# Two graph and mixture-of-experts layers: where the second choices are sent, and how the experts' tiles are cut

## The reference, cut to what matters

```
x = x + gnn0(layernorm(x), adj)     # in the eigenbasis of the adjacency's Laplacian
x = x + ffn0(layernorm(x))          # 8 experts, silu(x w1) * (x w3), then w2; top 2 by softmax
x = x + gnn1(layernorm(x), adj)     # graph convolution, two batch norms
x = x + ffn1(layernorm(x))          # a shared expert, and 8 experts with gelu and biases; top 2
```

## Time and profile before

| | |
|---|---|
| median of 3 runs | 1472.82 us (1469.61 to 1474.72) |
| the profiled execution | 1468.22 us, its span 1466.4 us |
| busy: PE, DVE, POOL, ACT | 77%, 62%, 45%, 38% of the span |
| chain of what ended last | PE 48%, issue 32%, another core or an unknown queue 7%, DVE 6% |
| costliest groups | write-backs L1462 (284 instructions, 300.9 us), sends L1016 (256, 257.7 us) |
| mean granted clock of PE | 0.922 |

### The profile page before, as it was taken

The page is one execution under the profiler, slowest core; times in us unless marked ns, Lnnn a source line. Parts: engine busy times, 40 slices in busy tenths (PEclk is TensorE's granted clock), DMA queues, the critical chain, the costliest instruction groups (busy, mean ns, idle before and its releaser), DMA issues.

```text
span 1466.4 us, 24078 instructions
## 1 busy us (share of the span) xinstructions
PE 1125.4 (77%) x6500; PEld 934.2 (64%) x6500; DVE 902.9 (62%) x3796; ACT 550.2 (38%) x1613; POOL 653.2 (45%) x675
## 2 busy tenths in 40 slices
PE   4555686388727978899999677999878877799990
PEld 3555575266615856688888443776657766699990
DVE  5776789767763544456676778887614433355673
ACT  3556567045511211122222365554323322244440
POOL 3000000054566666665444840044546666656664
PEclk9999999999958998899999798899989988899995
DMA  9993000001112222222242600011112222222436
GB/s 230 428 427 146 1 1 1 0 1 34 37 48 70 72 63 62 64 65 60 84 119 70 229 18 15 5 34 33 39 45 66 68 62 64 62 68 70 131 104 229
DMA packets 59270, 125.58 MB, mean 86 GB/s; under 512 B 13132, under 2 KB 39637, under 8 KB 57600
## 3 DMA queue, kind: packets, MB, share of 16 engines
q0 software_dynamic: 20000, 73.21, 13.2%
q1 hardware_dynamic: 39136, 50.84, 12.9%
HBM read 50.83 MB, written 74.99 MB: 86 GB/s over the span
## 4 chain that ended last, share of the span: by engine, by line
PE 48%; issue 32%; another core or an unknown queue 7%; DVE 6%; ACT 2%; DMA 2%; SPq 2%; POOL 1%; DVEq 0%; POOLq 0%; ACTq 0%
PE bank L1619 15%; PE bank L1610 9%; PE bank L1608 6%; PE bank L1607 6%; PE bank L1828 3%; PE bank L1836 3%; PE bank L1787 2%; PE bank L1595 2%; DMA u<-planes 1%; DVE bnh L1684 1%; PE bank L861 1%; SPq L2148 1%; DVE bn L1123 1%; ACT pay L1903 1%
## 5 line engine op out<-in xcount | busy, mean ns | idle before, releaser
L1462 POOL DMA_INDIRECT planes<-work,goal x284 | 300.9, 1059 | 211.0 <-DVE work L1531 124.2
L1016 POOL DMA_INDIRECT rows<-pay,slot x256 | 257.7, 1007 | 245.4 <-issue 78.3
L1619 PE MATMUL bank<-pay 128*128 128x128 f32 (+1 forms) x1988 | 297.7, 290 | 66.1 <-issue 34.0
L1619 PEld LDWEIGHTS bank<-pay 128*128 128x128 f32 (+1 forms) x1988 | 272.4, 199 | 95.3 <-issue 44.4
L1579 ACT ACTIVATE pay<-bank,pay 128x256 f32<-128x256 f32 x284 | 127.1, 475 | 211.3 <-PE bank L1610 123.9
L1575 ACT ACTIVATE pay<-bank 128x256 f32<-128x256 f32 (+1 forms) x213 | 81.1, 383 | 301.7 <-PE bank L1608 224.1
L1610 PE MATMUL bank<-pay 128*128 128x256 f32 x568 | 145.5, 402 | 3.0 <-issue 1.6
L1552 DVE TENSOR_TENSOR pay<-pay,bank 128x256 f32<-128x256 f32 (+1 forms) x213 | 88.6, 418 | 86.6 <-ACT pay L1575 44.5
L1607 PE MATMUL bank<-pay 128*128 128x256 f32 (+1 forms) x426 | 134.2, 398 | 7.6 <-issue 7.0
L1608 PE MATMUL bank<-pay 128*128 128x256 f32 (+1 forms) x426 | 131.7, 392 | 0.0
L195 PE MATMUL bank<-u 63*64 63x2 f32 (+61 forms) x496 | 73.7, 255 | 67.2 <-DVE u L180 66.1
(11 more groups left out here) (416 smaller groups left out, 2013.2 us busy)
## 6 DMA issues: line engine op xcount, KB each, us to landing
rows<-pay POOLq DMA_DIRECT2D x10, 3432.0 KB, 56.3
pay<-rows SPq DMA_DIRECT2D x142, 130.0 KB
u<-planes SPq DMA_DIRECT2D x64, 256.0 KB, 5.0
planes<-work,goal POOLq DMA_INDIRECT x284
wreg<-in_w SPq DMA_DIRECT2D x1, 4264.0 KB, 24.4
wreg<-in_w SPq DMA_DIRECT2D x1, 4112.0 KB, 13.3
X<-in_x SPq DMA_DIRECT2D x2, 2048.0 KB, 20.0
rows<-pay,slot POOLq DMA_INDIRECT x256
```

Source lines behind the costliest of these rows:

```text
L1016: return self.nc.gpsimd.indirect_dma_start(out=xs, out_offset=bass.IndirectOffsetOnAxis(ap=self.t["slot"][:, k, q:q + 1], axis=0), in_=sel ...
L1462: nc.gpsimd.indirect_dma_start(out=planes, out_offset=bass.IndirectOffsetOnAxis(ap=t["goal"][:, j * 2 + h:j * 2 + h + 1], axis=0), in_=t[" ...
L1619: ins = T.matmul(ps[4 + j % 2][:, h * P:(h + 1) * P], t["hh"][c][0:n, h * P:(h + 1) * P], t["wst"][j % 2][0:n, at + c * P:at + (c + 1) * P ...
```

## The change

- **The table's layout.** Each expert now owns `CAP` = 16640 rows. First choices go upwards from its middle (`CAP * e + 8192`), second ones downwards below it (their slots are counted negative and turned round in `place`). So second slots are final at once, `second_slots` is gone, and `clear_rows` has 20 blocks for 10.
- **The second sends.** They no longer belong to `experts_pool`. The new `send_seconds` marks a group (iota, copy, wait) and sends its 8 x 128 rows. In layer 1 two of them are sent behind each group of firsts from the second on (`BESIDE`); all that remain, 64 in layer 0 and 50 in layer 1, follow the last group at once. `experts_pool` then only writes back, one tile after another as they are ready, with `LANES` = 8 semaphores for 3 and `RING` = 16 for 18.
- **The tiles.** 57 tiles have 256 rows of one expert, 11 are split: two halves of 128 rows, of two experts. That is `NT` = 68 tiles and `NS` = 79 weight sets, for which `wst` has 4 buffers (`WAYS`). The order is 25 tiles of first choices, the 11 split ones, the other 32. A split tile has two row loads, two weight copies, twice the up products on half the columns, and in layer 1 two gelus and two bias additions for one. `table` is rewritten for the new list, with rounding by a large number in place of the 768-wide comparison.
- **The early plane** is fetched from tile `EARLY` = 62 on, with 8 semaphores for 4; what doesn't fit into the loop is fetched and added behind it.

```diff
-NT = (2 * TOKENS + E8 * (TS - 1)) // TS
-CAP = TOKENS + TS
+WHOLE = -(-(2 * TOKENS - E8 * (TS - 1)) // TS)
+MIXED = (2 * TOKENS + E8 * (P - 1)) // P - 2 * WHOLE
+MIXED += MIXED % 2
+NT = WHOLE + MIXED // 2
+NS = WHOLE + MIXED
+FIRSTS = (TOKENS + E8 * (TS - 1)) // TS + 1 + MIXED // 2
+CAP = 2 * TOKENS + TS
...
-BLOCKS = 10
-EARLY = 54
-RING = 18
-FREE = 8
-SENDS = 3
-BEHIND = 14
+BLOCKS = 20
+EARLY = 62
+RING = 16
+LANES = 8
+WAYS = 4
+BESIDE = (0, 2)
...
+    def send_seconds(self, pool, count, xs):
+        for q in range(self.seconds, min(N, self.seconds + count)):
+            g, first = divmod(q, GQ)
+            if first == 0:
+                pool.wait_ge(self.s(f"sent{g}"), 16 * GQ * (self.layer + 1))
+                qs = slice(q, q + GQ)
+                self.nc.gpsimd.iota(self.t["payi"][:, qs, P], ...).then_inc(self.s("marked"), 1)
+                self.nc.gpsimd.tensor_copy(self.t["pay"][:, qs, P + 1], self.t["gate2"][:, qs]).then_inc(...)
+                pool.wait_ge(self.s("marked"), self.past("marked", 2 * (g + 1)))
+            self.send(q, 1, xs).then_inc(self.s("sent_second"), 16)
+            self.seconds = q + 1
...
     for g in range(GROUPS):
         route.scatter(pool, g, xs, ready, rest)
+        if g:
+            route.send_seconds(pool, BESIDE[0], xs)     # BESIDE[1] in gnn1_pool
+    route.send_seconds(pool, N, xs)
...
+def split(j):
+    return PURE <= j < PURE + MIXED // 2
...
-    j = 0
-    if route.split:
-        pool.wait_ge(S("route_second"), sum(SPLIT[:layer + 1]))
-        route.mark_second(pool)
-        for q in range(FREE):
-            route.send(q, 1, xs).then_inc(S("route_sent_second"), 16)
-        for k in range(-(-(N - FREE) // SENDS)):
-            pool.wait_ge(s("xt"), past("xt", k + 1))
-            for q in range(FREE + k * SENDS, min(N, FREE + (k + 1) * SENDS)):
-                route.send(q, 1, xs).then_inc(S("route_sent_second"), 16)
-            if k >= BEHIND:
-                give_back(j)
-                j += 1
-        while j < k:
-            k += 1
-            pool.wait_ge(s("xt"), past("xt", k + 1))
-            give_back(j)
-            give_back(j + 1)
-            j += 2
-    for j in range(j, NT):
+    for j in range(NT):
         give_back(j)
...
     def weights(j):
-        expert = dve.value_load(t["expert"][j:j + 1, 0:1], min_val=0, max_val=E8 - 1)
-        if j >= 2:
-            dve.wait_ge(s("down"), past("down", j - 1))
+        for n in sets_of(j):
+            expert = dve.value_load(t["expert"][n:n + 1, 0:1], min_val=0, max_val=E8 - 1)
+            if n >= WAYS:
+                dve.wait_ge(s("down"), past("down", tile_of(n - WAYS) + 1))
...
+        for k, set_no in enumerate(sets_of(j)):
+            w = t["wst"][set_no % WAYS]
+            to = slice(k * P, (k + 1) * P) if split(j) else slice(0, TS)
+            ins = T.matmul(ps[c][0:n, to], w[:, a:a + n], x[:, to], start=True, stop=True)
...
     finish(NT - 1)
+    for T in range(NT - EARLY - 1, TILES):
+        add_plane(V, dve, S, t, layer, T, "early")
```

More of the change, by code:

```diff
@@ L736 @@
 E8 = 8
+ROUND = float(3 << 22)
 HID0 = 341
@@ L910, in choose @@
         dve.wait_ge(own.sem, n)
[L911 to L914, removed]
+        n = 2 * E8 * GQ
+        marks, i, e = r["o"], r["i"], r["e"]
         n = own.inc(V.tensor_tensor_scan(i, self.K[:, K_RESET:K_RESET + n], marks, 0.0, ALU.mult, ALU.add))
@@ L966, in place @@
             dve.wait_ge(own.sem, n2)
[L967 removed]
+            V.tensor_reduce(self.t["slot"][:, 1, qs], group(r["b"]), AX.X, ALU.add).then_inc(s("slots"), 1)
     def gates(self, dve, own, g, beside=lambda k: None):
@@ L1020, in all_sent @@
     def all_sent(self, eng):
-        eng.wait_ge(self.s("sent"), sum(SENT[:self.layer + 1]))
+        for g in range(GROUPS):
+            eng.wait_ge(self.s(f"sent{g}"), 16 * GQ * (self.layer + 1))
     def table(self, dve, own):
-        V, K, c, S, s = self.nc.vector, self.K, self.t["rc"], self.S, self.s
-        tb = self.t["tb"]
-        parts = 3 if self.split else 1
-        n = parts * E8
-        count, k, end, start, u, m, e, f = (tb[name][:, 0:n] for name in ("n", "k", "end", "start", "u", "m", "e", "f"))
@@ L1058, in table @@
-        own.chain(V.tensor_tensor_scan(end, self.t["ones"][:, 0:n], k, 0.0, ALU.mult, ALU.add))
-        own.chain(V.tensor_tensor(start, end, k, ALU.subtract))
-        own.inc(V.tensor_scalar(m, start, j, None, ALU.is_le))
-        if self.split:
-            own.chain(V.tensor_tensor(start, start, f, ALU.subtract))
-        own.chain(V.tensor_scalar(u, start, -float(TS), j256, ALU.mult, ALU.add))
-        own.chain(V.scalar_tensor_tensor(out=m, in0=end, scalar=j, in1=m, op0=ALU.is_gt, op1=ALU.mult))
@@ L1073, in table @@
-        with self.nc.allow_low_precision(reason="whole numbers below 2**24"):
-            V.tensor_reduce(self.t["first"], u, AX.X, ALU.add).then_inc(s("first"), 1)
-            own.chain(V.tensor_reduce(self.t["expert"], e, AX.X, ALU.add))
-        if self.split:
-            self.second_slots(own, count[:, E8:2 * E8], one_base, tb["f"][:, 0:E8], tb["look"])
+        V, K, s, tb = self.nc.vector, self.K, self.s, self.t["tb"]
+        n, f, w, z = tb["n"], tb["f"], tb["w"], tb["z"]
+        begin, end, much, at, u, m = (tb[name] for name in ("begin", "end", "much", "at", "u", "m"))
@@ new lines, in table @@
+        own.inc(V.tensor_tensor(f[:, e1], f[:, e1], m[:, half], ALU.mult))
+        own.chain(V.tensor_tensor(u.rearrange("p (k e) -> p k e", e=E8), m.rearrange("p (k e) -> p k e", e=E8), number, ALU.mult))
+        with self.nc.allow_low_precision(reason="whole numbers below 2**24"):
+            V.tensor_reduce(self.t["first"], at, AX.X, ALU.add).then_inc(s("first"), 1)
+            own.inc(V.tensor_reduce(self.t["expert"], u, AX.X, ALU.add))
+        own.chain(V.tensor_reduce(tb["v"], f[:, e1], AX.X, ALU.add))
@@ L1435, in experts_sp @@
     for j in range(NT):
-        if route.split and j == PURE:
-            sp.wait_ge(S("route_sent_second"), 16 * N * sum(SPLIT[:layer + 1]))
-        at = sp.value_load(t["first"][j:j + 1, 0:1], min_val=0, max_val=E8 * CAP - TS)
+        if j == PURE:
+            sp.wait_ge(S("route_sent_second"), SENT * (layer + 1))
+        ats = [sp.value_load(t["first"][n:n + 1, 0:1], min_val=0, max_val=E8 * CAP - TS) for n in sets_of(j)]
         if j >= 4:
```

341 lines of the change are left out of this document (180 added, 161 removed).

## The result

The change made the kernel 1.6% slower: 1497.09 us (median of 4 runs, 1493.43 to 1499.43) against 1473.61 (4 runs, 1469.61 to 1474.72); ratio 1.0163, 95% interval 1.0133 to 1.0194. The forecast was 1446. The profiled execution took 1499.43 us (span 1497.6, mean clock 0.889).

What follows compares the result with a forecast made beforehand. TensorE bounds late tiles; POOL's pauseless indirect DMAs, delaying others' semaphores, slow each layer's first 32. Terms 4 - 32 + 3 - 24 + 15 + 7 = -27 us take the profiled 1468.2 to 1441, median 1446; range 1400 to 1482.

Steps and rivals of the forecast that it cites:

- The bulk sends: Second sends issued together after the last first sends, then pauseless write-backs: layer 0 +4 us, layer 1 -32 us.
- p: Progress of the other engines while POOL issues without pause, 1 being undisturbed; 0.5 for sends, 0.4 for pauseless write-backs.
- the burst of 14: Fourteen sends in a row in layer 0 of the kernel before, 439.81 to 457.5 us; progress 0.45 over 17 us.
- burst freezes all: Rival: other engines nearly stand still during the bulk (p near 0.1); +23 us, 1496; chance 0.15.
- The moved sends: 14 second sends put into layer 1's routing stage, where POOL was said to have room: +3 us (0 to 10).
- Tiles: Expert loops: 71 tiles become 68, three fewer in each layer: -24 us.
- Split tiles: Eleven tiles of two experts, a second weight copy partly showing on DVE: +15 us (2 to 27).
- Loop ends: End of each expert loop: eleven early-plane adds follow the last tile, 3.6 us later twice: +7 us (2 to 14).
- At nothing: Routing table, doubled clearing, more weight buffers and write-back lanes priced at no cost; table +3 if bared, clearing 0 to 2.
- the shared expert went on: Evidence against the freeze: layer 1's shared expert progressed over eight sends, 1071.8 to 1081.7 us, after a pause.
- equal shares: Rival: every DMA of a burst costs its share however placed; only tiles and ends remain, -2 us, 1471; chance 0.08.
- short pauses suffice: Rival: short pauses between groups of bulk sends keep p at 0.8 to 0.9; -68 us, 1405; chance 0.22.

Runs made afterwards that it cites:

- e1: Kernel before with all 64 second sends of a layer issued at once, then the write-backs: 1497.85 us, ratio 1.0162.
- e4: Kernel after with POOL pausing (a copy and a wait for it) behind every second send of the closing run: 1518.08 us.
- e7: Kernel after with POOL pausing (a copy and a wait) behind every fourth of the closing second sends: 1460.62 us.
- e12: Kernel after with no second sends moved into layer 1's routing stage, all 64 in the closing run: 1484.58 us, ratio 1.0084.
- e14: Kernel after with pauses at every fourth send and write-back (tiles 0 to 39), all groups' first sends, and ahead of each moved pair: 1414.83 us, ratio 0.9625.
- e8: Kernel before with a pause ahead of every fourth first send of groups 5 to 7: 1462.96 us, ratio 0.9943.
- e11: Kernel before with 64 second sends at once and pauses every fourth DMA in late first sends, second sends and write-backs: 1432.61 us, ratio 0.9729.
- e5: Kernel after with four empty POOL instructions behind every closing second send, which vanished in the gap between sends: 1496.36 us.
- e6: Kernel after with POOL pausing (a copy and a wait) behind every two of the closing second sends: 1476.23 us.
- e16: e14 with write-backs of tiles 0 to 59 pausing at every second DMA (layer 0) or third (layer 1): 1358.1 us, ratio 1.0252.
- e13: Kernel after with no second sends moved and pauses every fourth DMA in late first sends, second sends and write-backs: 1422.78 us, ratio 0.9667.
- e15: e13 with the pause after every third indirect DMA instead of every fourth: 1426.62 us, ratio 0.9682.

## Why the prediction was wrong

**The bulk sends: the step that failed.** I took a progress of p = 0.5 for sends in eights with 1.5 us between, as nearer the burst of 14. The mean over a burst of 17 us (0.45) hid that nothing much is late in its first half and nearly everything in its second; ACT went idle at 448.6, in the middle of that burst. I stretched the mean over the whole bulk. Measured: 3 tiles in 86 us, that is (8 + 2 x 4.22) / 86 = 0.19, where I had 0.5 and 8.6 tiles. The delay set in after some 10 DMAs and didn't clear at the marks. The rival "burst freezes all", 1496 at a chance of 0.15, was the right mechanism: tile 33 of layer 0 came at 677.8, +31, where it had +23. Some 7 us of that is the same delay a little earlier: in a run of 18 first sends DVE waited 8.59 us for a product of PE (until 426.78; 1.61 for the same one in the kernel before), and the bulk began at 446.58 and not near 439. In layer 1 the routing's tail and tiles 0 to 33 together took 19.9 us more than before (12 for the moved sends and some 4 for splits and loop end among them), where I had -32 for the burst and the rival -4. e1 shows that this term alone costs what the whole change cost, e4 to e7 that it is the run.

**The moved sends** were sized +3 (0 to 10) on "there is room"; by e12 they cost 12, past the dear end, because they lengthen runs (e14). The margin is the interval's, 4 us or so.

**Tiles** -24: right (22.5 less in the "33 to last" columns, with two split tiles in each). **Split tiles** +15 was too dear: 6.2, near the low end of 2; most of the second weight copy is hidden. **Loop ends** +7: 4.7. **At nothing**: clearing right (POOL's memset moved from 202 to 209 us, nothing waited). The routing table was not free in layer 1's run of sends: it waits for DVE's own signals (up to 2.26 us).

The account of the loss: bulk +25 (e1), moved sends +12 (e12), tiles, splits and ends -13: +24, and 23.5 were measured. It is an estimate: e1's bulk has no marks, and 64 sends in layer 1 for 50. Of the 51 us between forecast and result the bulk is 53 (-28 forecast, +25 measured) and the moved sends 9; the split tiles and loop ends, priced too dear, give 11 back. What I weighed against the freeze, that the shared expert went on over eight sends after a pause, was the right row read the wrong way: eight after a long pause are short of the run that hurts.

**The price per DMA** ("equal shares") was a rival at 0.08 and is refuted; "short pauses suffice" had the right idea (0.22) but a pause every eight sends is too rare and one every four enough for most of it; with those the new kernel came to 1415 to 1431, above its 1405.

## What to carry to other kernels

Where POOL issues indirect DMAs beside other engines' work, look for runs. The signs are ACT and DVE idle on a product that PE has made, "remote" in the waits, and often a release just behind the run's end. A forced stop of 0.8 us every four DMAs is a cheap thing to try: it gave 0.6% on the first sends of the kernel before (e8), 2.7% in all its places with the bulk (e11), and the new kernel with stops in all places had the lowest ratio of the first five occasions (e14, 0.9625, measured on one of them). Then measure on more than one occasion: on the sixth the trouble was absent from the traces, and the kernels with bulk sends and stops were 2 to 2.5% slower than the kernel before. And never carry the mean of a short burst over a long one; ask what its second half looked like.

## What the runs showed of the hardware

- POOL's indirect DMAs of 128 rows (0.98 us, 0.30 between) in a run of more than about ten hold back PE's completions as ACT and DVE see them. ACT stood idle up to 24 us for one in the kernel after (21 of them after the product was made), and 39, 36 and 31 in e1, e5 and e7. The release came 1.4 to 8 us after the run or well inside a long one. Sends to the table and write-backs do it alike (e4, e6). DVE's own completions were late by up to 3.6 us (e7). ACT's completions reached PE at once. Here is e5 in its run, then e7 behind 24 sends, 16 of them first ones, that had no pause:
```profile
512.96 0.38 ACT L1597 ACTIVATE work<-bank 128x256 f32<-128x256 f32 x1 [36.13 <-remote]
```
```profile
1104.26 0.69 ACT L1928 ACTIVATE work<-bank,wreg 128x512 f32<-128x512 f32 x1 [30.97 <-remote]
```
- The Trainium skill ("DMA: Bandwidth & Descriptors", Anatomy of one DMA) says that many descriptors can be emitted before the incremental cost shows. That is said of the descriptors of one DMA, and every send here has 128 rows, so no run tests it; the prediction stretched it to a row of DMAs. POOL itself kept 1.28 us a DMA from the first to the 64th, and the cost fell on the others.
- One occasion of six ran the kernel before 10% faster and the paused ones 4% faster than their like elsewhere, at the same POOL durations (mean 1.00 us a send in e14, 1.01 in e16). What differed is open; the chip number was that of e13 to e15. How the kernel after would stand there was not run.
- What holds the completions back (a queue, a port, event traffic) is open: sends of fewer rows or bytes were not tried. The mean rate of the DMAs alone it isn't, by e7 against the kernel after.
